# Attention and FP4 feed-forward in one kernel: a new order within the pairs of heads, fewer key tiles summed by GpSimd, and moved waits at a batch's end

## The chip, the cores and the metric

One core of one Trainium2 chip. The metric is the device time of one execution in microseconds, the median of several runs. The engines are TensorE (matmuls; PE, its weight loads PEld), VectorE (DVE), ScalarE (ACT), GpSimd (POOL) and SyncE (SP), which issues most DMAs.

## The reference

```python
# x: (8, 1024, 512) fp32, 16 heads of 32, F = 1408
xn  = layernorm(x)                                   # no scale, no shift, eps 1e-5
qkv = xn @ W_attn + b_attn
att = softmax(where(causal, q @ k.T * 32 ** -0.5, -inf))
x + (att @ v) @ W_proj + b_proj                      # attention
  + fp4(silu(fp4(xn) @ fp4(w_gate).T) * (fp4(xn) @ fp4(w_up).T)) @ fp4(w_down).T
# fp4: blocks of 16, scale = max|.| / 6, nearest of 0 .5 1 1.5 2 3 4 6
```

## The kernel before, in words

The kernel goes through eight batches of attention and then through a loop of 64 token tiles of the feed-forward part, which the change leaves as it is. fp32 products of accuracy are made of high and low halves in a rounded fp32 format.

A batch has three stages. First the projections (`PROJ`) make q, k and v; q and k go through DRAM and come back as stacks of a pair of heads. Then come eight pairs of heads. Then the end of the batch: the output projection (`output`), the additions (`add`), the quantisation of two of the feed-forward weight tiles beside it (`scale_unit`, `round_unit`, `transpose_unit`, `high_of_unit`, `low_of_unit`, `store_unit`), and the first four x tiles of the next batch (`transpose_x`, `low_of_x`).

A pair's work on TensorE, for eight key tiles of 128 keys:

- Row scores (`scores`, line 1189, step T): 16 tiles a pair, 128 queries by up to 1024 keys, whose row maxima VectorE takes (`row_max`, line 761). They are made for the pair ahead. Two may be under way. Their odd ones and the denominators share a bank.
- The step MAX (`maxima`, line 1194) transposes the maxima. VectorE splits them (`split_max`, lines 767 and 769), SyncE writes both halves into the pair's stack by two DMAs (line 521), and the pair's first transposed score waits for these (line 1209).
- Transposed scores (`transposed_scores`, line 1216, steps S0 to S3 of a row): keys by queries, with the maximum already subtracted. A row stands for one key tile and has 4 parts (rows 0 to 3), 2 (rows 4 and 5) or one for both heads (rows 6 and 7). They go round three banks: a part waits for the exp of the part three before. Parts on the diagonal get a mask matmul in bf16 (`mask_transposed`, lines 1225 and 1228, steps M). ScalarE takes exp (line 1066).
- Products with V (`times_v`, line 1242, steps P0 to P7, by key tile): four column tiles of the array at once, by head and by parity of the query tile. A key tile whose number isn't below its row's belongs to the pair before.
- Denominators (`denominators`, lines 1254 and 1261, step DEN, for the pair before): GpSimd sums the exps of key tiles (lines 686 and 688, `summed(p)` tiles of pair p); matmuls by ones sum over the keys, and the tiles that GpSimd leaves out are added by matmuls of ones on the exps themselves. VectorE copies the result (line 778), SyncE spreads it over the partitions (line 571), VectorE inverts (line 782), SyncE writes and broadcasts the inverse (lines 576 and 581), and VectorE divides (`divide`, line 798).

The order is written out by hand: `STEPS` has one string for each row on TensorE, gone through once per pair; `VECTOR_STEPS` is VectorE's order (R a row maximum, Y0 and Y1 the two halves of a division of the pair before last, DEN the copy, INV the inversion, MAX the split). Each engine works strictly in its order. A loop of a pair here is the time from its first transposed score to the next pair's.

```python
pe.wait_ge(m_in, ONE + b * PAIRS * 2 * DMA + (p + 1) * 2 * DMA)   # ahead of S0 of row 0
```

Of the kernel before, what the change touches and what calls it, by code (L numbers as in the profile page):

```python
# [45 lines left out]
def attention(nc, ctx, banks, memory, shared, x, w_attn, b_attn, w_proj, b_proj, w_gate, w_up, w_down, qk_scratch, ones_scratch,  # L46
# [5 lines left out]
    ST = S // P  # L52
    HG = P // HD
    G = HEADS // HG
    PAIRS = HEADS // 2
# [18 lines left out]
    ST_RING, SLOTS, XR, RES = 3, 4, 4, 6  # L74

    RINGED = 5
# [5 lines left out]
    TAIL0 = {kt: 2 * P * sum(ST - k for k in range(RINGED, kt)) for kt in range(RINGED, ST)}  # L82
    TAIL = 2 * P * sum(ST - k for k in range(RINGED, ST))

    def summed(p):

        return ST if p < PAIRS - 2 else RINGED if p < PAIRS - 1 else 3

    SUM_ORDER = [*range(1, ST)]
    FREED = {0: 1, 1: 1, 2: 2, 3: 3, 4: 4}
# [6 lines left out]

    STEPS = ["T T S0 S1 T P3 T S2 S3 T M2 M3",
# [7 lines left out]


    VECTOR_STEPS = "R R R R R R R Y0 Y1 DEN R R R R R R INV MAX R R R"
    FLAT = " ".join(STEPS).split()
    EARLY = TILES - FLAT[:FLAT.index("MAX")].count("T")

# [181 lines left out]
    SPLIT = G - 1  # L297
# [409 lines left out]
    def vector(dve):  # L707
# [46 lines left out]
        def body(b, final):  # L754
# [46 lines left out]
            def low_of_y(g):  # L801
                dve.wait_ge(y_hi, ONE + b * SPLIT * 2 + (g + 1) * 2)
                nc.vector.tensor_tensor(yt_low[:, g], yt[:, g], yt_high[:, g].bitcast(F32), ALU.subtract).then_inc(y_lo_first, 1)  # L803

            def add(k):

                if k >= 2:
                    dve.wait_ge(o_out[k % 2], ONE + b * (ST // 2) * DMA + (k // 2) * DMA)
                elif k == 0:
                    dve.wait_ge(y_div, ONE + b * PAIRS * 2 + PAIRS * 2)  # L810
                dve.wait_ge(o_res, ONE + b * ST + k + 1)
                filled(dve, b, "P", k)
                nc.vector.tensor_tensor(ob[:, k % 2], bank("P", k), res_tile(k, final), ALU.add).then_inc(o_sum, 1)
# [44 lines left out]
            def low_of_unit(i):  # L858
                n = turn(b, i)
                dve.wait_ge(q_out[i % 2], ONE + slot_turns(b, i) * 2 * DMA)  # L860
                dve.wait_ge(q_hi, ONE + n + 1)
                nc.vector.tensor_tensor(unit_space[i % 2][:, 4].bitcast(F32R), ps_y[:, :], unit_space[i % 2][:, 3],
                                        ALU.subtract).then_inc(q_lo, 1)
# [44 lines left out]
            for p in range(PAIRS):  # L908
                for step in VECTOR_STEPS.split():
                    if step == "R":  # L910
                        tile, due = tile_of(due), due + 1
                        if (1, AHEAD_OF_ALL) <= tile < (PAIRS, 0):
                            row_max(*tile)
                    elif step == "DEN":
                        if p:
                            copy_den(p - 1)
                    elif step == "INV":
                        if p == PAIRS - 1 and not final:

                            for g in range(SPLIT - 1):  # L920
                                low_of_y(g)
                        if p:
                            invert(p - 1)
                        if p == PAIRS - 1 and not final:
                            for t in range(XR):
                                norm(b + 1, t)
                        if p == PAIRS - 1 and final:

                            shared.quantise_first(dve)
                    elif step == "MAX":  # L930
                        if p + 1 < PAIRS:
                            split_max(p + 1)
                        if p == PAIRS - 2 and not final:
                            for t in range(XR):
                                stats(b + 1, t)
                    elif p > 1:
                        divide(p - 2, [int(step[1])])
# [1 line left out]
            invert_last()  # L939
            divide(PAIRS - 1)  # L940
            if not final:
                for t in range(XR):
                    low_of_x(b + 1, t)
            else:
                shared.low_of_first(dve)
            one, two = beside_projection(final)
            for k in range(ST):
                add(k)
                if k == 0:
                    scale_unit(one)  # L950
                if k == 1:
                    round_unit(one)
                if k == 2:
                    scale_unit(two)
                if k == 3:
                    round_unit(two)
                if k == 5:
                    low_of_unit(one)
                if k == 7:
                    low_of_unit(two)  # L960

        batches_in_line(body)

    def scalar(act):
# [16 lines left out]
        def body(b, final, rest):  # L981
# [11 lines left out]
            def high_of_unit(i):  # L993
                n = turn(b, i)
                act.wait_ge(q_out[i % 2], ONE + slot_turns(b, i) * 2 * DMA)
                act.wait_ge(q_full, ONE + n + 1)
                nc.scalar.activation(unit_space[i % 2][:, 3].bitcast(F32R), ps_y[:, :], ACT.Copy).then_inc(q_hi, 1)

            def store_unit(i):
                matrix, u = unit_of(b, rest, i)  # L1000
                act.wait_ge(q_lo, ONE + turn(b, i) + 1)
                for half in range(2):
                    act.dma_start(wq[half, :, matrix * FC + u], unit_space[i % 2][:, 3 + half]).then_inc(q_out[i % 2], DMA)

            for kind, i in PROJ:
# [19 lines left out]
                g, r, _ = QK[i]  # L1025
# [64 lines left out]
            one, two = beside_projection(final)  # L1090
            for k, t in enumerate(OUT):
                act.wait_ge(o_sum, ONE + b * ST + k + 1)
                act.dma_start(acc[b, t * P:(t + 1) * P, :], ob[:, k % 2]).then_inc(o_out[k % 2], DMA)
                if k + (2 if final else RES) < ST:
                    load(k + (2 if final else RES))
                if k == 0:
                    magnitudes(one)
                if k == 2:
                    magnitudes(two)
                if k == 4:  # L1100
                    high_of_unit(one)
                if k == 6:
                    high_of_unit(two)
                    store_unit(one)
            store_unit(two)

        batches_and_rest_in_line(body)

    def tensor(pe):
        pe.wait_ge(consts, 2)  # L1110

        def transpose_x(b, t):

            pe.wait_ge(t_lo, ONE + b * ST + max(t - ST_RING + 1, 0))
            pe.wait_ge(normed, ONE + b * ST + t + 1)
            for k in range(KC):
                last = nc.tensor.transpose(x_bank(t)[:, k * P:(k + 1) * P], xs[:, t % XR, k * P:(k + 1) * P],
                                           ident[:, :])
            last.then_inc(t_full, 1)
# [10 lines left out]
        def body(b, final):  # L1130
# [115 lines left out]
            def denominators(p):  # L1246
                pe.wait_ge(summed_up, ONE + b * SUMS + SUMS0[p] + summed(p) - 1)
                pe.wait_ge(first_sums, ONE + b * PAIRS + p + 1)
                if p + 2 < PAIRS:

                    pe.wait_ge(s_max, ONE + b * PAIRS * TILES + (p + 2) * TILES + AFTER_DEN // 2 * 2)
                for s in range(2):
                    for h in range(2):
                        last = nc.tensor.matmul(by_tile(den_bank(p)[y_rows(h, s)]), ones[:, :], by_tile(sums(p, h, final))[:, s::2],  # L1254
                                                start=True, stop=summed(p) == ST)
                for kt in range(summed(p), ST):
                    for s in range(2):
                        if parity_tiles(kt, s) >= ST:
                            continue
                        for h in range(2):  # L1260
                            last = nc.tensor.matmul(by_tile(den_bank(p)[y_rows(h, s), y_cols(kt, s)]), ones[:, :],
                                                    exps_of_parity(kt, h, s), start=False, stop=kt == ST - 2 + s)
                last.then_inc(den_full, 1)
# [79 lines left out]
            for k in range(OUT_BANKS):  # L1343
                pe.wait_ge(y_div, ONE + b * PAIRS * 2 + (PAIRS - 2 + min(k, 1)) * 2)
                emptied("P", k)
                output(k, range(G - 1))
            if not final:
                transpose_x(b + 1, XR - 1)
            pe.wait_ge(y_div, ONE + b * PAIRS * 2 + PAIRS * 2)
            one, two = beside_projection(final)  # L1350
            for k in range(ST):
                if k < OUT_BANKS:
                    output(k, [G - 1])
                else:
                    emptied("P", k)
                    output(k, range(G))
                if k == 4:
                    transpose_unit(one)
                if k == 6:
                    transpose_unit(two)  # L1360

        batches_in_line(body)

# [452 lines left out]
```

## Time and profile before

| what | value |
| --- | --- |
| median of 3 runs | 3576.71 us (3575.12 to 3578.76) |
| profiled execution | 3577.77 us, span 3575.8 us |
| granted TensorE clock | 0.999 of full speed |
| TensorE busy | 3510.3 us (98%) |
| VectorE busy | 2688.8 us (75%) |
| ScalarE busy | 1217.6 us (34%) |
| GpSimd busy | 1103.0 us (31%) |

The shares are over the whole span. The eight batches take about 2016 us of it, the feed-forward loop the rest; GpSimd works in the first part alone. Matmuls are pipelined and their ends are modelled, so the time that a step takes on TensorE is read from the starts of two neighbours. A wait is put down to the instruction whose signal came last.

### The profile page before, as it was taken

To read this page: it belongs to the slowest core of one execution; us is meant where nothing else is said; L and a number is where in the kernel's file an instruction comes from. 1 tells how busy PE (TensorE), PEld (TensorE's weight loads), DVE (VectorE), ACT (ScalarE), POOL (GpSimd) and SP (SyncE) were. 2 spreads that over 40 slices of the span, in tenths; PEclk is the share of its full clock that TensorE was granted. 3 is DMA by queue.
4 is the path that set the end of the run, shared out by engine and by line. 5 is a ranking of instruction groups with operands and counts; after the bars stand their busy time and mean duration, and the time that the engine had idled before them with its cause. 6 is when DMAs were issued, how large, how long until landed. Compare 5 with 4: busy or idle time off the path is not lost.

```text
span 3575.8 us, 55225 instructions
## 1 busy us (share of the span) xinstructions
PE 3510.3 (98%) x19892; PEld 2607.0 (73%) x19892; DVE 2688.8 (75%) x4872; ACT 1217.6 (34%) x2292; POOL 1103.0 (31%) x552
## 2 busy tenths in 40 slices
PE   8999999999999999999999999999999999999999
PEld 6557567566576575675665688888888888888887
DVE  6786876877877768778777677777777777777776
ACT  2542543534615525435335222222222222222222
POOL 1770952934817709529338100000000000000000
PEclk9999999999999999999999999999999999999999
DMA  6535446346365355363465410110110110110010
GB/s 220 133 100 188 105 146 172 83 154 170 82 197 133 109 180 116 134 183 83 139 189 161 177 32 29 35 35 27 35 35 26 35 35 28 34 35 31 31 35 30
DMA packets 182895, 348.94 MB, mean 98 GB/s; under 512 B 42960, under 2 KB 50640, under 8 KB 181840
## 3 DMA queue, kind: packets, MB, share of 16 engines
q1 hardware_dynamic: 158256, 291.75, 28.4%
q10 hardware_dynamic: 24480, 55.06, 4.3%
q8 instruction: 101, 1.65, 0.2%
q14 instruction: 58, 0.48, 0.0%
HBM read 225.19 MB, written 120.00 MB: 97 GB/s over the span
## 4 chain that ended last, share of the span: by engine, by line
PE 78%; DVE 6%; issue 6%; POOL 3%; DMA 3%; ACT 2%; SPq 1%; ACTq 0%; POOLq 0%; DVEq 0%
PE f_ps L1691 27%; PE f_ps_o L1703 13%; PE ps_dense L1164 12%; PE ps_st L1216 6%; PE ps_s L1189 5%; PE ps_dense L1242 3%; PE ps_y L1242 3%; POOL stage L688 2%; PE ps_dense L1254 2%; PE f_ps L1683 2%; PE ps_dense L1189 1%; POOL stage L686 1%; DVE yt_low L803 1%; PE ps_dense L1330 1%; PE ps_st L1225 1%
## 5 line engine op out<-in xcount | busy, mean ns | idle before, releaser
L1691 PE MATMUL f_ps<-wgu,xqt 128*128 128x512 f32 (+1 forms) x4608 | 990.2, 372 | 1.7 <-DVE xqt L1546 1.4
L1691 PEld LDWEIGHTS f_ps<-wgu,xqt 128*128 128x128 f32 x4608 | 840.4, 188 | 122.7 <-DVE xqt L1546 1.6
L1066 ACT ACTIVATE pt<-ps_st 128x512 f32<-128x512 f32 (+3 forms) x1152 | 543.6, 525 | 448.8 <-PE ps_st L1216 306.8
L761 DVE CUSTOM_DVE_ANT_0 ps_s<-ps_s,row_mask 128x640 f32<-128x640 f32 (+3 forms) x512 | 529.9, 1035 | 126.8 <-PE ps_s L1189 122.6
L1703 PE MATMUL f_ps_o<-wd,hqt 128*128 128x512 f32 x2112 | 512.1, 395 | 0.6 <-DVE hqt L1572 0.6
L1703 PEld LDWEIGHTS f_ps_o<-wd,hqt 128*128 128x128 f32 x2112 | 392.0, 188 | 79.4 <-DVE hqt L1572 0.8
L1164 PE MATMUL ps_dense<-arena,wa 128*128 128x512 f32 x1536 | 378.2, 395 | 0.3 <-DVE stage L818 0.3
L686 POOL TENSOR_TENSOR stage<-pt 128x1792 f32<-128x1792 f32 x41 | 164.9, 4021 | 564.2 <-ACT pt L1066 546.0
L1164 PEld LDWEIGHTS ps_dense<-arena,wa 128*128 128x128 f32 x1536 | 284.8, 188 | 60.9 <-issue 3.8
L688 POOL TENSOR_TENSOR stage<-stage,pt 128x1536 f32<-128x1536 f32 (+2 forms) x107 | 321.4, 3004 | 15.7 <-ACT pt L1066 8.2
L1216 PE MATMUL ps_st<-arena 98*128 98x512 f32 (+3 forms) x768 | 247.4, 390 | 4.7 <-ACT pt L1066 2.2
L761 DVE CUSTOM_DVE_ANT_0 ps_dense<-ps_dense,row_mask 128x128 f32<-128x128 f32 (+3 forms) x424 | 219.0, 516 | 40.0 <-PE ps_dense L1189 38.2
L1216 PE MATMUL ps_st<-stack 98*128 98x512 f32 (+3 forms) x768 | 242.9, 382 | 3.2 <-DMA stack<-mr 2.6
L1636 ACT ACTIVATE silu<-f_ps 128x512 f32<-128x512 f32 (+1 forms) x192 | 107.1, 558 | 369.3 <-PE f_ps L1691 369.2
L1216 PEld LDWEIGHTS ps_st<-arena 98*128 98x128 f32 x768 | 136.6, 191 | 88.6 <-ACT pt L1066 46.0
L1631 ACT ACTIVATE ha<-ht 128x1408 f32<-128x1408 f32 x63 | 87.1, 1382 | 325.2 <-DVE ht L1467 325.2
L1028 ACT ACTIVATE stage<-ps_dense,bqk 128x512 fp32r<-128x512 f32 x128 | 88.0, 688 | 314.0 <-PE ps_dense L1164 297.6
L1565 DVE TENSOR_TENSOR h<-silu,f_ps 128x512 f32<-128x512 f32 (+1 forms) x192 | 122.7, 639 | 92.1 <-ACT silu L1636 88.6
L1164 PE MATMUL ps_dense<-wa,arena 128*128 128x512 f32 x768 | 187.5, 394 | 0.0
L1216 PEld LDWEIGHTS ps_st<-stack 98*128 98x128 f32 x768 | 138.2, 192 | 66.2 <-ACT pt L1066 30.3
L1470 DVE SCALAR_TENSOR_TENSOR hd<-ha,ht 128x1408 f32<-128x1408 f32 (+1 forms) x65 | 104.2, 1603 | 91.9 <-ACT ha L1631 91.2
L818 DVE SCALAR_TENSOR_TENSOR stage<-ps_dense,bqk,stage 128x512 fp32r<-128x512 f32 x128 | 95.9, 749 | 101.6 <-ACT stage L1028 101.6
(166 smaller groups left out, 5425.1 us busy)
## 6 DMA issues: line engine op xcount, KB each, us to landing
qk_scratch<-stage SPq DMA_DIRECT2D x128, 512.0 KB, 3.0
stack<-qk_scratch SPq DMA_DIRECT2D x192, 256.0 KB
arena<-qk_scratch SPq DMA_DIRECT2D x192, 256.0 KB
xs<-in_L_attn_x SPq DMA_DIRECT2D x64, 256.0 KB, 3.8
acc_scratch<-rob ACTq DMA_DIRECT2D x64, 256.0 KB, 2.0
xt<-in_L_attn_x SPq DMA_DIRECT2D x64, 256.0 KB, 2.6
at<-acc_scratch SPq DMA_DIRECT2D x64, 256.0 KB, 2.7
out<-ot SPq DMA_DIRECT2D x64, 256.0 KB, 2.0
```

The source lines that it names most:

```text
L686: nc.gpsimd.tensor_tensor(both[:, :, cols], exps(0)[:, :, cols], exps(1), ALU.add).then_inc(summed_up, 1)
L688: nc.gpsimd.tensor_tensor(both[:, :, cols], both[:, :, cols], exps(kt), ALU.add).then_inc(summed_up, 1)
L761: nc.vector.tensor_tensor_reduce(row, row, row_mask[:, S - keys:S], -1.0, LARGEST, ALU.add, ALU.min, mx[:, h * ST + q:h * ST + q + 1]).the ...
L1066: nc.scalar.activation(exps(kt)[:, heads[0], q - kt * P:q - kt * P + n], ps_st[:, w % ST_RING, 0:n], ACT.Exp, scale=SCALE).then_inc(st_exp, 1)
L1164: last = nc.tensor.matmul(bank(*use), left(lh, k), right(rh, k), start=n == 0, stop=n == len(terms) - 1)
L1189: last = nc.tensor.matmul(out[:, k0:k1], qs, stack(p)[0:KS, 2 + h, k0:k1], start=True, stop=True)
L1216: last = nc.tensor.matmul(ps_st[:, w % ST_RING, j * n:(j + 1) * n], stack(p)[0:KM, 2 + h, kt * P:(kt + 1) * P], stack(p)[0:KM, h, q:q + n] ...
L1242: last = nc.tensor.matmul(by_tile(y_bank(p)[y_rows(h, s), y_cols(kt, s)]), v_head(kt, p, h), exps_of_parity(kt, h, s), start=kt == 0, stop ...
L1565: nc.vector.tensor_tensor(h[:, f:f + n], silu[:, c, 0:n], ps[:, SLOT[c], 1, 0:n], ALU.mult).then_inc(h_mul, 1)
L1636: nc.scalar.activation(silu[:, c, 0:n], ps[:, SLOT[c], 0, 0:n], ACT.Silu).then_inc(s_done, 1)
L1691: last = nc.tensor.matmul(ps[:, SLOT[c], gu, 0:n].rearrange("p (j n) -> p j n", n=P), xqt[:, a, k], wgu[:, b, gu * FC + f // P:gu * FC + ( ...
L1703: last = nc.tensor.matmul(ps_o[:, :], hqt[:, a, k], wd[:, b, k], start=i == 0, stop=i == len(terms) - 1)
```

## The change

It writes `STEPS` and `VECTOR_STEPS` anew. MAX goes from the end of row 3 to the start of row 5, DEN from row 2 to the start of row 3, the products of P3 and P4 of the pair before go together at the end of row 0, P5, P6, P7 in row 1, and the row-score tiles T are spread otherwise: three come behind MAX where five did. GpSimd sums 8, 7, 8, 7, 7, 6, 5, 3 key tiles in the pairs 0 to 7 instead of 8, 8, 8, 8, 8, 8, 5, 3. At the end of a batch VectorE makes only one of its two low halves of y ahead of the last inversion from DRAM, the fourth x tile's transposition and low half come after the first output tile, and the second weight tile's transposition and its halves move behind the eight outputs; the first one's halves are taken one step earlier.

```diff
+    SUMMED = (8, 7, 8, 7, 7, 6, 5, 3)
     def summed(p):
-        return ST if p < PAIRS - 2 else RINGED if p < PAIRS - 1 else 3
+        return SUMMED[p]

-    STEPS = ["T T S0 S1 T P3 T S2 S3 T M2 M3",
-             "S0 P5 T T S1 S2 S3 M2 M3 T",
-             "S0 DEN P6 P7 P0 S1 T S2 S3 T M2 M3 T P1 T T",
-             "S0 S1 P2 S2 M2 S3 M3 MAX",
-             "S0 T M0 S1 M1",
-             "S0 T M0 S1 T M1",
-             "S0 P4 M0",
-             "S0 M0"]
-    VECTOR_STEPS = "R R R R R R R Y0 Y1 DEN R R R R R R INV MAX R R R"
+    STEPS = ["S0 S1 S2 M2 T S3 T M3 P3 P4 T",
+             "T S0 S1 S2 T P5 P6 P7 M2 T S3 M3",
+             "S0 T S1 S2 T S3 M2 M3",
+             "DEN P0 T T S0 S1 S2 P1 T T M2 S3 M3",
+             "S0 T M0 S1 M1 P2",
+             "MAX S0 T M0 S1 M1",
+             "S0 M0 T",
+             "S0 M0 T"]
+    VECTOR_STEPS = "R R R R Y0 R R R Y1 R DEN R R R R R INV MAX R R R"
...
 # VectorE, step INV of the last pair, not in the final batch
-                            for g in range(SPLIT - 1):
-                                low_of_y(g)
+                            low_of_y(0)
                         if p:
                             invert(p - 1)
                         if p == PAIRS - 1 and not final:
+                            for g in range(1, SPLIT - 1):
+                                low_of_y(g)
                             for t in range(XR):
                                 norm(b + 1, t)
...
 # VectorE, end of the batch
-                for t in range(XR):
+                for t in range(XR - 1):
                     low_of_x(b + 1, t)
...
             for k in range(ST):
                 add(k)
+                if k == 0 and not final:
+                    low_of_x(b + 1, XR - 1)
...
-                if k == 5:
+                if k == 4:
                     low_of_unit(one)
-                if k == 7:
-                    low_of_unit(two)
+            low_of_unit(two)
...
 # ScalarE
-                if k == 4:
+                if k == 3:
                     high_of_unit(one)
                 if k == 6:
-                    high_of_unit(two)
                     store_unit(one)
+            high_of_unit(two)
             store_unit(two)
...
 # TensorE, denominators
-                                                start=True, stop=summed(p) == ST)
+                                                start=True, stop=summed(p) >= ST - 1 + s)
...
 # TensorE, output projection
-            if not final:
-                transpose_x(b + 1, XR - 1)
...
+                if k == 0 and not final:
+                    transpose_x(b + 1, XR - 1)
                 if k == 4:
                     transpose_unit(one)
-                if k == 6:
-                    transpose_unit(two)
+            transpose_unit(two)
```

## Rows read from the trace of the kernel before

**Rows 1.** the page: busy us of each engine (share of the span), instructions
```profile
PE 3510.3 (98%) x19892; PEld 2607.0 (73%) x19892; DVE 2688.8 (75%) x4872; ACT 1217.6 (34%) x2292; POOL 1103.0 (31%) x552
```

**Rows 2.** windows, batch 2: us; busy PE, PEld, DVE, ACT, POOL (count); clock, DMA, GB/s
```profile
611.57:630.30 18.73, 17.93 (x133) 10.07 (x132) 13.74 (x37) 10.44 (x24) 17.64 (x9) 1.00 0.60 135
648.17:666.04 17.87, 17.87 (x133) 10.01 (x132) 15.17 (x39) 10.46 (x24) 16.62 (x8) 1.00 0.46 107
...
701.75:719.31 17.56, 16.82 (x125) 8.85 (x124) 14.56 (x42) 11.72 (x27) 16.52 (x8) 1.00 0.25 71
...
739.10:767.90 28.80, 26.58 (x113) 18.98 (x114) 22.86 (x33) 4.63 (x8) 10.06 (x8) 1.00 0.59 203
```

**Rows 3.** waits of the whole span: engine and line, releaser; us in total, times, longest
```profile
PEld ps_s L1189 <- DVE mx L761: 109.3, 205, 0.8
...
PE ps_dense L1254 <- POOL stage L688: 8.7, 14, 1.4
```

**Rows 4.** timeline of TensorE, pair loop 3 of batch 2: start us, us, instructions
```profile
649.74 0.73 PE L1189 MATMUL ps_s<-stack 96*128 96x512 f32 x2
650.31 0.64 PE L1216 MATMUL ps_st<-arena 98*128 98x512 f32 x2
650.78 0.23 PE L1189 MATMUL ps_dense<-stack 96*128 96x128 f32 x1
...
654.25 1.07 PE L1254 MATMUL ps_dense<-stage,ones 128*32 128x512 f32 x8
655.13 0.62 PE L1242 MATMUL ps_dense<-rob,v 128*32 128x128 f32 x12
...
661.73 0.28 PE L1194 MATMUL ps_dense<-ident,mx 128*128 128x128 f32 x1
...
662.08 0.45 PE L1189 MATMUL ps_s<-stack 96*128 96x512 f32 x2
662.37 0.23 PE L1225 MATMUL ps_st<-identb,causal 128*128 128x128 bf16 x1
...
662.77 0.42 PE L1216 MATMUL ps_st<-arena 98*128 98x384 f32 x1
...
664.47 0.64 PE L1242 MATMUL ps_y<-pt,v 128*32 128x256 f32 x8
665.04 0.28 PE L1228 MATMUL ps_st<-identb,causal 128*128 128x256 bf16 x1
...
665.38 0.42 PE L1189 MATMUL ps_dense<-stack 96*128 96x384 f32 x1
...
666.04 0.63 PE L1216 MATMUL ps_st<-stack 98*128 98x512 f32 x2
```

**Rows 5.** timeline of VectorE and of SyncE, same loop; DMA issues: KB, us to landing
```profile
662.04 0.28 DVE L767 CAST mr<-ps_dense 16x128 fp32r<-16x128 f32 x1 [0.35 <-PE ps_dense L1194]
...
656.26 3.08 SPq L571 DMA_DIRECT2D den<-rob  x4
...
662.66 1.17 SPq L521 DMA_DIRECT2D stack<-mr  x2
...
stack<-mr SPq DMA_DIRECT2D x64, 8.0 KB, 2.1
arena<-mr SPq DMA_DIRECT2D x64, 8.0 KB, 1.8
```

**Rows 6.** timeline of TensorE, pair loop 6 of batch 2
```profile
715.86 0.28 PE L1194 MATMUL ps_dense<-ident,mx 128*128 128x128 f32 x1
...
719.30 0.50 PE L1216 MATMUL ps_st<-arena 98*128 98x512 f32 x1
```

**Rows 7.** timeline of ScalarE, pair loop 3 of batch 2
```profile
657.09 0.60 ACT L1066 ACTIVATE pt<-ps_st 128x512 f32<-128x512 f32 x1 [2.05 <-PE ps_st L1216]
```

**Rows 8.** timeline of VectorE and of TensorE at the end of batch 1
```profile
480.02 7.31 DVE L803 TENSOR_TENSOR yt_low<-yt,stack 128x1024 fp32r<-128x1024 f32 x2
...
517.07 0.66 PE L1201 MATMUL ps_y<-ident,pt 128*128 128x128 f32 x4 [1.32 <-DVE pt L862]
```

## The prediction

> **What bounds the kernel now.** I read the engine shares first: TensorE is busy 98% of the span, VectorE 75%, GpSimd 31% [rows 1]. The reader should see that only time that TensorE gains or loses can move the end. The change touches the attention part alone, so next I read windows cut at the starts of the pairs' transposed scores, in batch 2: pair loop 1 takes 18.73 us, a steady loop (3) 17.87 with TensorE busy in all of it, loop 6 17.56, the batch's end, from the last denominators to the next batch's first product, 28.80, of which TensorE is busy 26.58 [rows 2]. The waits come third: TensorE's largest are weight loads of row scores behind a row maximum (109.3 us in 205 waits, mostly hidden under the matmul before) and denominators behind GpSimd's sums (8.7 us in the open) [rows 3]. Last the timeline of one steady pair, because a busy share can't say how near a hidden wait is to showing [rows 4, 5].
>
> **The chain that the new order uncovers.** A pair's first transposed score needs the row maxima: the transposition MAX on TensorE, cast and subtraction on VectorE, two DMAs issued one behind the other by SyncE, their landing. In the steady pair MAX starts at 661.73 [rows 4], the cast at 662.04, the first DMA is issued at 662.66, and both issues take 1.17 us, so the second starts 0.59 later [rows 5]. A DMA from mr lands 1.8 us (arena slots) or 2.1 us (stack slots) after its issue in the median [rows 5]. Sum: 0.93 + 0.59 + 1.8 to 2.1 = 3.3 to 3.6 us. The next pair's S0 starts at 666.04, 4.31 us after MAX, so some 0.8 us of cover is left over. Loop 6 shows the chain bare: MAX at 715.86, S0 at 719.30, 3.44 us, with less work behind MAX [rows 6]. I take 3.5 us: this, and a little for a weight load that waits itself and then shows.
>
> The Trainium skill (DMA: Bandwidth & Descriptors, the section on the two cost components of a DMA) gives a fixed cost of about 2.0 us whatever the size. By that figure, as an estimate, the chain is 0.2 us longer than with the arena row's 1.8 and the sum below some 10 us higher; loop 6's bare chain speaks against it, and I don't use it.
>
> In the old order MAX closes row 3. In the new one it opens row 5, behind row 4's scores, masks and P2. What stood behind MAX and no longer does, by the starts in the steady pair [rows 4]: S4.0, S4.1 and their masks 0.72 (from 661.76, just behind MAX, to 662.77, less T0, 662.08 to 662.37), P4 0.57 (664.47 to 665.04) and 0.10 for entering it, and the row-score tiles T3 and T4 0.66 (665.38 to 666.04), which the new order puts behind S0. 4.31 - 2.05 = 2.26 us of work is left against a chain of 3.5: TensorE stands 1.24 us before each pair. Nothing can pass the waiting S0: all of TensorE's later work is queued behind it, and with it the exps, the row maxima and the sums. 3.4 us is the least that the wait's end can come after MAX by these rows; with traffic a landing can be later.
>
> **What the new order saves.** (a) One visit to the V products fewer (6 to 5: P3 P4, P5 P6 P7, DEN P0, P1, P2); the column work of the visits together is the same. A visit's edges: DEN, two passes of 512 columns, takes 0.88 (654.25 to 655.13), so P4's two passes of 256 are 0.44, and it takes 0.57: 0.13 to leave it. The first tile behind a visit takes 0.57 for 1024 columns (649.74 to 650.31) where two other scores of 512 take 0.47 (650.31 to 650.78): 0.10, since its weights load in the open. I take the same 0.10 for V's weights at the visit's start. Together 0.33 us a pair [rows 4]. (b) 205 weight loads wait for a row maximum, over three a pair [rows 3]; where such a load shows it costs that 0.10. The new places give VectorE more time ahead of most tiles and part the two divisions: some 0.3 to 0.4 a pair. (c) Against that, new waits. S0.3 stands three scores behind S0.0 and needs its exp: 0.4 for the score to end, 0.6 for an exp of 512 columns [rows 7] and 0.1 of signals and load, against 1.0 us of work between: 0.1. T11 needs the copy of the denominators, which had P6, P7, P0 and S2.1 as cover and now has P0 alone: up to 0.1. Net of (a), (b), (c), with a little for fewer masks ahead of scores: 0.6 us saved, between 0 (all of (b) comes back as other waits, and some of (a)) and 0.95.
>
> A steady loop: 17.87 - 0.6 + 1.24 = 18.5, so +0.63 us.
>
> **GpSimd's sums.** Pairs 1, 3 and 4 leave out key tile 7, pair 5 tiles 6 and 7; TensorE adds them as matmuls of ones. Two passes of 128 columns are 0.22 by DEN's 0.88 for 512 [rows 4]; tile 7 is one such, tiles 6 and 7 two: 3 x 0.22 + 0.44 = 1.1 us a batch, all on the path, since DEN stands ahead of MAX. GpSimd is busy 16.6 of 17.87 us in a steady pair [rows 2], which an 18.5 us pair relieves anyway, so I count nothing won there (0 to -0.2 a pair). What goes is DEN's wait for GpSimd in loop 1, as DEN stands some 2 us later: loop 1 is 0.86 over the steady one [rows 2], and 8.7 us of such waits in 8 batches [rows 3] agree with it: -0.85 a batch.
>
> **Sum of the pairs, per batch.** Loops 1 to 5: 5 x 0.63 = 3.15. Ones: 1.1. DEN in loop 1: -0.85. Loop 0: the 0.72 of row 4 comes ahead of MAX and the 4.3 behind it shrinks to 3.5: 0. Loop 6 was bound by the chain before, so all that moves ahead of MAX or behind S0 counts: 0.72 + 0.67 + 0.66 - 0.6 = +1.45. Loop 7 gets P4 of pair 6 and is bound by exps otherwise: +0.3 (0 to 0.6). Late landings, which 0.8 us of cover used to hide: 0.06 a pair, 0.4. Together 5.5 us a batch, 44 us in 8.
>
> **The batch's end.** (d) VectorE makes one low half of y, then the inversion, then the other. Both took 7.31 us ahead of the inversion (from 480.02) [rows 8], which now comes some 3 us earlier, and with it the division of pair 6, the last reciprocal, the last division and the first addition, the latter by 1 to 2 us, until the last denominators bind. (e) The fourth x tile's transposition no longer stands between the first output groups and the last, and the second unit's transposition goes behind output 7: its wait of 1.32 us for the first unit's low half (517.07) [rows 8] goes, as that low half also comes one addition earlier. TensorE idles 2.2 us in this stage (28.80 - 26.58) [rows 2]; I take 1.8 back in 7 batches and 1.0 in the last: -13.6 us. The bounds are 0 and -18. That the second unit's high and low halves now end later, ahead of the next batch's first copies on ScalarE and VectorE, costs nothing while the next batch's first products (12 matmuls of 512 columns, 2.8 us by the 0.47 for two) cover them; without that cover it costs 1 us a batch.
>
> Total: 44 - 13.6 = +30.4 us on the profiled execution's 3577.8 (span 3575.8), 3608.2. The median of the runs shown is 1.1 below that execution: 3607 us.
>
> **Rivals.**
> 1. The first score doesn't wait: the maxima land sooner, or TensorE's work behind MAX is longer than I count. A steady pair is then 17.27 us and a batch 5 x -0.6 + 1.1 - 0.85 + 0.3 = -2.5; 8 x -2.5 - 13.6 = -34: 3543 us. For it: one visit fewer, and TensorE is the bound. Against it: loop 6 has this very wait now. It decides from a chain below 2.3 us; the total breaks even at one of 2.95. Chance 0.06.
> 2. VectorE is held at the inversion when MAX comes. From DEN to MAX there is 6.9 us of work in the new order (DEN and P0 1.9, T11 and T12 0.75, S3.0 to P1 1.8, T13 and T14 0.7, S3.3 to the last mask of row 4 1.0, P2 0.78). The denominators' first DMA is issued 2.0 us after DEN's start (656.26), the four issues take 3.08 us [rows 5], a landing some 1.8: 6.3 to 6.9. Where these are late the cast waits, and S0 with it: 0.3 to 0.5 us in half of the pairs, 10 to 15 us in all: 3620 us. Chance 0.14.
> 3. The savings cover the wait: 0.95 a pair (-17 us), all of 18 at the batch's end, loop 7 unchanged (-2): 44 - 17 - 2 - 18 = +7: 3583 us. Chance 0.05.
> The forecast itself: 0.75.
>
> **Numbers.** Range 3585 to 3630: the lower end by savings of 0.95 a pair and some more at the batch's end, the upper by savings near 0.2 a pair (+19) or rival 2. No change is within 0.2%, 7 us, about what a measurement of this kernel can tell. Faster 0.06, same 0.04, slower 0.90.
>
> **What would show it.** From MAX to the next pair's first score 3.4 to 3.6 us in every pair, TensorE idle for some 1.2 us there and the wait put down to the DMA from mr; steady loops of 18.3 to 18.7; a loop 6 near 19; no wait of DEN for GpSimd; more idle time on GpSimd and VectorE per pair; a batch's end near 27 us without the 1.3 us ahead of the unit's transposition. I am wrong if that first score starts at once, or if steady loops come under 17.9.

## The result and the profile after

The changed kernel takes 3666.3 us (median of 4 runs, 3662.9 to 3672.4) against 3577.0 for the kernel before beside it: ratio 1.0252, interval 1.0234 to 1.0269. It is slower, as forecast, but by 89 us and not by 30, outside the range of 3585 to 3630. The profiled execution took 3672.4 us, 94.6 more than that of before.

The page has the busy us of each engine, then the granted clock in 40 slices. TensorE has 192 matmuls more than in [rows 1], of 128 columns each, and is busy 39 us longer. The row of the granted clock shows a 9 in every slice, as that of the kernel before does, so the page hides what happened:

```profile
PE 3549.2 (97%) x20084; PEld 2664.6 (73%) x20084; DVE 2682.3 (73%) x4872; ACT 1217.0 (33%) x2292; POOL 1072.1 (29%) x512
...
PEclk9999999999999999999999999999999999999999
```

The windows answer to [rows 2]. Batch 5 is the one in which only loop 7 was disturbed. In order: loops 1, 2, 3, 6, 7 and the end of batch 5, then loops 2 and 3 of batch 2, and a stretch of 3.2 us in batch 1 (columns as in [rows 2]; the granted clock is the third number from the right):

```profile
1420.51:1439.09 18.58, 17.59 (x132) 10.39 (x132) 13.94 (x38) 10.46 (x23) 17.55 (x9) 1.00 0.59 132
1439.09:1457.91 18.82, 17.81 (x136) 10.71 (x136) 15.01 (x40) 10.46 (x23) 16.16 (x7) 1.00 0.44 101
1457.91:1476.84 18.93, 17.60 (x132) 10.39 (x132) 15.16 (x40) 10.46 (x23) 16.74 (x8) 1.00 0.43 100
1514.60:1534.15 19.55, 17.54 (x139) 10.18 (x139) 15.07 (x44) 12.42 (x27) 17.48 (x7) 1.00 0.23 70
1534.15:1555.54 21.39, 21.06 (x207) 11.63 (x208) 10.72 (x15) 11.28 (x25) 13.05 (x6) 0.92 0.30 99
1555.54:1582.78 27.24, 27.09 (x115) 19.28 (x116) 23.51 (x34) 4.03 (x7) 10.10 (x8) 1.00 0.58 203
...
660.53:680.93 20.40, 19.40 (x135) 11.26 (x135) 15.01 (x40) 10.46 (x23) 16.13 (x7) 0.92 0.40 93
680.93:701.43 20.50, 19.16 (x132) 10.91 (x132) 15.18 (x40) 10.46 (x23) 16.73 (x8) 0.92 0.39 93
...
385.60:388.80 3.20, 3.20 (x19) 1.75 (x20) 1.48 (x4) 0.60 (x1) 3.04 (x3) 0.50 1.04 225
```

The same loop 2 takes 18.82 us at a clock of 1.00 and 20.40 at 0.92. The last row shows where such a mean comes from: for 3.4 us the clock is granted at half, the 1.2 GHz level, and 3.4 x 0.5 / 20.4 is the 8% that loop 2 lacks. The pair loops of this trace hold 30 such stretches, of 3.4 us or twice that, 119 us in all; those of the kernel before hold none.

The waits of the whole span (us, times, longest) answer to [rows 3]. The new ones are the 32 + 24 = 56 first scores, and the weight loads behind the copy of the denominators. The 205 weight loads of row scores into ps_s that waited for a row maximum have become 9; those into ps_dense, 41 before, are 90:

```profile
PE ps_st L1217 <- DMA arena<-mr: 44.4, 32, 3.1
PE ps_st L1217 <- DMA stack<-mr: 28.9, 24, 3.0
...
PEld ps_dense L1190 <- DVE mx L761: 64.4, 90, 0.8
...
PEld ps_s L1190 <- DVE mx L761: 6.2, 9, 1.7
...
PEld ps_dense L1190 <- DVE rob L778: 48.6, 48, 1.3
...
PE ps_dense L1190 <- DVE rob L778: 2.9, 8, 0.4
```

TensorE's timeline of pair loop 3 in batch 5 answers to [rows 4]: denominators, P0, the tile behind it (T11), MAX, the last tile ahead of the next pair, and the next pair's first score:

```profile
1466.19 1.06 PE L1255 MATMUL ps_dense<-stage,ones 128*32 128x512 f32 x8
1467.08 1.04 PE L1243 MATMUL ps_y<-pt,v 128*32 128x512 f32 x8
1468.48 0.45 PE L1190 MATMUL ps_dense<-stack 96*128 96x384 f32 x1 [0.36 <-DVE rob L778]
...
1473.39 0.33 PE L1195 MATMUL ps_dense<-ident,mx 128*128 128x128 f32 x1
...
1475.28 0.60 PE L1190 MATMUL ps_s<-stack 96*128 96x512 f32 x2
1476.84 0.96 PE L1217 MATMUL ps_st<-stack 98*128 98x512 f32 x3 [0.96 <-DMA stack<-mr]
```

From MAX to the first score it is 3.45 us, as worked out, with 0.96 us of idle time at its end. VectorE and SyncE in the same loop, which answer to [rows 5]: a row maximum, the denominators' copy, the cast behind MAX, the DMAs:

```profile
1466.76 0.97 DVE L761 CUSTOM_DVE_ANT_0 ps_s<-ps_s,row_mask 128x768 f32<-128x768 f32 x1
...
1467.74 0.69 DVE L778 COPY rob<-ps_dense 128x512 f32<-128x512 f32 x1
...
1473.76 0.28 DVE L767 CAST mr<-ps_dense 16x128 fp32r<-16x128 f32 x1 [0.44 <-PE ps_dense L1195]
...
1474.38 1.17 SPq L521 DMA_DIRECT2D stack<-mr  x2
```

Last, the same visit P3 at both clock levels: in batch 5, and in batch 2, 2.66 us behind a first score (680.93) that had waited 0.96 us:

```profile
1460.10 1.28 PE L1243 MATMUL ps_dense<-pt,v 128*32 128x256 f32 x16
```
```profile
680.93 0.96 PE L1217 MATMUL ps_st<-arena 98*128 98x512 f32 x3 [0.96 <-DMA arena<-mr]
...
683.59 2.36 PE L1243 MATMUL ps_dense<-pt,v 128*32 128x256 f32 x16
```

**Where the 94.6 us are.** An undisturbed batch is 148.8 us from its first score to its last denominators (15.34, 18.58, 18.82, 18.93, 18.82, 18.94, 19.55, and 19.85 for loop 7, which the fill run below shows at full clock) against 142.8 before: 6.05 x 8 = 48. The batch's end, to the next batch's first score, went from a mean of 104.7 to 102.8 us in seven batches: -13.6 in sum. Clock: a disturbed loop 2 is 1.58 us longer (20.40 - 18.82) for its 3.4 us at the low level; 119 / 3.41 x 1.58 = 55. The rest, 5, is about what late first scores leave: in this trace they came, in sum, 13.6 us later than 3.45 us after MAX, and the kernel before has some 6 us of longer loops of its own. My terms were 44, -13.6, none, and 3 within the 44. The 55 is an estimate, as it prices every low stretch like that of loop 2.

### The profile page after: what moved, and what is told of

It reads as the page before. It is cut to its first block, busy times and chain, and to the rows that moved or that the text cites. A ratio compares the mean times of both kernels' runs of the same rounds, so it can differ in the third digit from the quotient of the medians.

```text
span 3670.6 us, 55494 instructions
## 1 busy us (share of the span) xinstructions
PE 3549.2 (97%) x20084; PEld 2664.6 (73%) x20084; DVE 2682.3 (73%) x4872; ACT 1217.0 (33%) x2292; POOL 1072.1 (29%) x512
## 4 chain that ended last, share of the span: by engine, by line
PE 86%; DVE 6%; DMA 4%; issue 2%; ACT 1%; SPq 1%; ACTq 0%; POOL 0%; POOLq 0%; DVEq 0%
PE f_ps L1691 26%; PE ps_dense L1165 14%; PE f_ps_o L1703 13%; PE ps_st L1217 7%; PE ps_dense L1243 4%; PE ps_s L1190 4%; PE ps_y L1243 4%; PE ps_dense L1331 3%; PE ps_dense L1190 2%; DMA arena<-mr 2%; PE f_ps L1683 1%; DMA stack<-mr 1%; PE ps_st L1226 1%; PE ps_dense L1255 1%; DVE ps_s L761 1%
## 5 line engine op out<-in xcount | busy, mean ns | idle before, releaser
L1217 PE MATMUL ps_st<-stack 98*128 98x512 f32 (+3 forms) x768 | 234.4, 383 | 31.3 <-DMA stack<-mr 28.9
L1217 PEld LDWEIGHTS ps_st<-arena 98*128 98x128 f32 x768 | 144.8, 200 | 109.0 <-DMA arena<-mr 53.7
L1217 PEld LDWEIGHTS ps_st<-stack 98*128 98x128 f32 x768 | 145.6, 197 | 71.8 <-DMA stack<-mr 36.7
L1226 PE MATMUL ps_st<-identb,causal 128*128 128x128 bf16 x768 | 166.2, 234 | 0.0
```

What stands on the lines that cost most here:

```text
L1217: last = nc.tensor.matmul(ps_st[:, w % ST_RING, j * n:(j + 1) * n], stack(p)[0:KM, 2 + h, kt * P:(kt + 1) * P], stack(p)[0:KM, h, q:q + n] ...
L1226: nc.tensor.matmul(ps_st[:, w % ST_RING, 0:P], causal[:, :], identb[:, :], start=False, stop=True).then_inc(st_full, 1)
```

## The experiments

**Fill the wait.** Does the low clock make the missing 60 us? Five matmuls of 512 columns run ahead of each pair's first score, into its own bank, which the score then overwrites. They need nothing that the score waits for but its bank, so the order and the landing stay as they are (MAX to the first score is 3.49 us).

```diff
                 w = p * NPARTS + PART0[kt] + i
+                if (kt, i) == (0, 0) and p:
+                    pe.wait_ge(st_exp, ONE + b * PAIRS * NPARTS + max(w - ST_RING + 1, 0))
+                    for _ in range(5):
+                        nc.tensor.matmul(ps_st[:, w % ST_RING, 0:512], stack(p)[0:KS, 2, 0:P], stack(p)[0:KS, 0, 0:512],
+                                         start=True, stop=True)
```

> The changed kernel, with five matmuls of 512 columns (1.15 us of TensorE) put ahead of each pair's first transposed score, into the bank which that score then overwrites: TensorE works through most of the 1.2 us in which it waited for the row maxima, and nothing gets there sooner. Theory A (the clock): the wait itself costs what was forecast, some 34 us with everything else in, and the rest of the 89 us, some 55, is the granted clock falling behind that wait. Then the granted clock comes back to 0.998 or more, steady loops are all 18.8 to 18.9 us, and the time is about 3612 us, 0.985 of the changed kernel, although TensorE has more to do. Rival B (the new order itself is longer on TensorE, or the clock falls for another reason): the time stays near 3666 us or rises by up to 60 us, and the clock stays near 0.985.

Measured: 3621.5 us (3619.5 to 3628.1), ratio 1.0123 (1.0106 to 1.0139). More work on TensorE made the kernel 45 us faster. The windows of loops 3 and 6 of batch 5 are within 0.1 us of those in the changed kernel, and the clock is full:

```profile
1426.67:1445.60 18.93, 18.56 (x137) 11.26 (x137) 15.17 (x40) 10.46 (x23) 16.78 (x8) 1.00 0.43 100
1483.36:1502.84 19.48, 18.71 (x144) 10.98 (x144) 15.01 (x44) 12.42 (x27) 17.45 (x7) 1.00 0.21 70
```

10.2 us at the low level are left in the pair loops, of 119. So the wait's length and the clock are two costs, and this takes away the second alone. The time is 9 us above the expected 3612; the stretches that are left make about 5 of them (10.2 / 3.41 x 1.58).

**The batch's end alone**, on the kernel before: the edits to low_of_y, low_of_x, transpose_x, high_of_unit, low_of_unit and transpose_unit, with all key tiles summed as before.

```diff
-            if not final:
-                transpose_x(b + 1, XR - 1)
...
+                if k == 0 and not final:
+                    transpose_x(b + 1, XR - 1)
                 if k == 4:
                     transpose_unit(one)
-                if k == 6:
-                    transpose_unit(two)
+            transpose_unit(two)
```

> The kernel before with the edits at the batch's end alone (old order, old sums). Theory A: 1.8 us less per batch end, 7 batches and about 1 us in the last: -13 us, 3564 us, clock 0.999. Rival: the end's later halves of the second weight tile delay the next batch's first copies, and the gain is under 4 us.

Measured: 3565.9 us (3561.3 to 3568.2), ratio 0.9968 (0.9955 to 0.998): -11.8 us against -13.6 worked out. The batch's end in batch 2, of 28.80 us in [rows 2], is

```profile
733.61:760.84 27.23, 27.01 (x115) 19.26 (x115) 22.02 (x31) 4.04 (x7) 10.04 (x8) 1.00 0.57 201
```

**A late maximum in the old order.** Three small DMAs to scratch in memory, issued by SyncE ahead of the two that the first score waits for, lengthen the chain and leave TensorE's order alone.

```diff
                 sp.wait_ge(m_lo, ONE + b * PAIRS + p + 1)
+                for j in range(3):
+                    sp.dma_start(mx_scratch[j], mr[:, j % 2].bitcast(F32)).then_inc(mx_out, DMA)
```

> The kernel before in its old order, with three more small DMAs (to a scratch in DRAM) issued ahead of the two that carry the row maxima: each takes the queue some 0.59 us, so the chain from MAX to the next pair's first score is some 5.2 us long against 4.3 us of cover. One suspected cost alone, without the new order. Theory A: the wait of some 0.9 us in loops 0 to 5 and 1.8 more in loop 6 makes 7.2 us a batch, 58 us at full clock (3635 us), and the granted clock falls behind such waits too, so 3650 to 3700 us at a clock of 0.98 to 0.99. Rival B (the clock falls for something in the new order, not for the wait): 3635 us at 0.998.

Measured: 3625.5 us (3618.3 to 3638.1), ratio 1.0129 (1.0112 to 1.0146). The three issues cost less than I took: MAX to S0 became 4.69 us, so a steady loop waits only 0.2 us. A batch of this trace at full clock throughout (the fourth) is 2.4 us longer than the same batch of the kernel before, so by its length the longer chain is worth 2.4 x 8 = 19 us. Of the 60 us by which the profiled execution is longer, the low level makes another 33, by the same price: 71.7 us in 9 stretches of up to 10.2 us. The remaining 8 lie in loops with later first scores. A loop at full clock and one with such a stretch:

```profile
664.28:682.60 18.32, 18.02 (x131) 9.94 (x132) 15.25 (x40) 10.45 (x23) 16.67 (x8) 1.00 0.46 106
623.45:646.09 22.64, 22.42 (x131) 12.09 (x132) 12.74 (x35) 10.56 (x23) 16.59 (x8) 0.77 0.49 109
```

The 31 first scores with a wait under 0.5 us never lowered it. Each stretch begins in or behind a wait of 1.0 to 1.8 us: seven times that of a late first score or of the one at loop 6's end, twice that of a row score for VectorE. The one above began 1.1 us behind this score:

```profile
623.45 0.73 PE L1220 MATMUL ps_st<-stack 98*128 98x512 f32 x2 [1.31 <-DMA stack<-mr]
```

**The same with two fill matmuls** ahead of each first score.

```diff
+                if (kt, i) == (0, 0) and p:
+                    ...
+                    for _ in range(2):
+                        nc.tensor.matmul(ps_st[:, w % ST_RING, 0:512], ...)
```

> e3's kernel (old order, maxima 0.4 us late for S0) with two matmuls of 512 columns (0.46 us) ahead of each pair's first transposed score. The chain and the loops stay as in e3 where the clock is full (18.22 us). Theory A: TensorE is no longer idle there, and the granted clock goes from 0.989 to 0.998 or more: the 72 us at the lower clock in e3's attention part cost about half, 30 to 36 us, less where they lay over waits, so 3590 to 3605 us. If the clock fell for another reason: 3625 us at 0.989.

Measured: 3619.4 us (3610.7 to 3622.5), ratio 1.0119 (1.0104 to 1.0135). By the medians the fill wins 6 us only, as the late maximum's runs differ much (and lie over this run's 3610.7 to 3622.5 in part): 3638.1, 3628.8, 3622.2 and 3618.3 us at mean clocks of 0.989, 0.992, 0.994 and 0.996. The profiled executions are the fastest of the one and the slowest of the other, so their difference is no measure of the edit, but it fits the price of the low level: 3610.7 us with 6.8 us at the low level against 3638.1 with 71.7, -27 us, where 64.9 / 3.41 x 1.58 = 30 were due. A steady loop and loop 7 of batch 5, the latter with the same 19.47 us as without the fill:

```profile
1389.83:1408.05 18.22, 18.22 (x135) 10.37 (x134) 15.03 (x39) 10.45 (x23) 16.61 (x8) 1.00 0.46 105
1481.10:1500.58 19.48, 19.36 (x199) 10.14 (x200) 11.29 (x10) 11.26 (x25) 12.95 (x6) 1.00 0.30 102
```

So the two matmuls fill the short waits to the end, cost nothing in a steady loop, and leave the length of the late chain as it is. As the short waits had not lowered the clock, what helps must be the longer ones: the wait at loop 6's end went from 1.10 to 0.64 us. With 6 us between the medians, this pair of runs supports the account of the clock by its traces and hardly by its times.

**P4 moved alone, five visits.** What is a visit to the V products worth?

```diff
-    STEPS = ["T T S0 S1 T P3 T S2 S3 T M2 M3",
+    STEPS = ["T T S0 S1 T P3 P4 T S2 S3 T M2 M3",
...
-             "S0 P4 M0",
+             "S0 M0",
```

> The kernel before with one edit: P4 moved from row 6 behind P3 in row 0 of the next loop, so that a pair has five visits to the V products, while MAX keeps 3.6 us of work behind it. If a visit's edges cost what I took (0.33 us a pair on the path), this is 56 x 0.33 = 18 us less, 3560 us. Rival C (the steady pair is held by the alternation of row scores and row maxima, so that time saved on TensorE elsewhere turns into a longer wait for VectorE at the next row-score tiles): less than 4 us of change, and more waiting of L1189 for L761.

Measured: 3586.3 us (3580.7 to 3590.4), ratio 1.0026 (1.0016 to 1.0036). That is 9 us more than the kernel before, where 18 less were expected. An undisturbed batch is 0.4 us longer, 3 us in eight; the profiled execution is the fastest of nine, the others stand at mean clocks down to 0.996, and what lengthens them was not traced. A steady loop is 17.91 us, none the shorter, and busy throughout:

```profile
648.65:666.56 17.91, 17.91 (x132) 10.36 (x132) 15.25 (x39) 10.35 (x23) 16.55 (x8) 1.00 0.46 107
```

Rival C of that expectation holds in its mechanism, though not in its size (under 4 us of change). P4's 0.67 us are gone from behind MAX, but MAX to S0 went from 4.31 to 4.06 only, because the tile ahead of the next pair waits for VectorE. VectorE's third row maximum behind MAX ends at 666.00, and the tile that needs its bank starts at 666.06 and not 0.25 us after the one before it, as in the kernel before (665.63, behind the 665.38 of [rows 4]):

```profile
664.98 0.97 DVE L761 CUSTOM_DVE_ANT_0 ps_s<-ps_s,row_mask 128x768 f32<-128x768 f32 x1
665.86 0.14 DVE L761 DVE_READ_ACCUMULATOR2_ANT mx<- 128x1 f32 x1
```
```profile
665.64 0.42 PE L1189 MATMUL ps_dense<-stack 96*128 96x384 f32 x1
666.06 0.67 PE L1189 MATMUL ps_s<-stack 96*128 96x512 f32 x2
```

The hidden waits of weight loads grew from 205 to 248 in number, with the same total ([rows 3]: 109.3 us):

```profile
PEld ps_s L1189 <- DVE mx L761: 108.7, 248, 0.8
```

**The order alone**: the new STEPS and VECTOR_STEPS on the kernel before, nothing else.

```diff
-             "S0 S1 P2 S2 M2 S3 M3 MAX",
+             "DEN P0 T T S0 S1 S2 P1 T T M2 S3 M3",
...
+             "MAX S0 T M0 S1 M1",
```

> The kernel before with the new STEPS and VECTOR_STEPS alone (old sums, old batch end). If the batch's end gives 12 us back wherever it stands, as e2 showed in the old order, and the sums of seven tiles cost 1.1 us a batch (9 us): 3666 + 12 - 9 = 3669 us, clock 0.984. If the sums cost nothing, since the ones fall where TensorE would wait for VectorE or for the maxima anyway: 3678 us.

Measured: 3679.7 us (3674.0 to 3687.7), ratio 1.0287 (1.0271 to 1.0303), 116 us at the low level in the pair loops. The order carries the whole loss, and the batch's end takes back its 12 us in the full change.

**The change with eight tiles summed** on GpSimd in all of pairs 0 to 5.

```diff
-    SUMMED = (8, 7, 8, 7, 7, 6, 5, 3)
+    SUMMED = (8, 8, 8, 8, 8, 8, 5, 3)
```

> The changed kernel with GpSimd summing all eight tiles in pairs 0 to 5, as before. My step: 1.1 us of ones a batch are on the path, so this is 9 us faster, 3657 us. Rival: the time is the same within 3 us (steady loops 18.82 and 18.93 as in the changed kernel), or it is slower, because DEN now waits for GpSimd's eighth sum.

Measured: 3676.7 us (3669.9 to 3681.9), ratio 1.0281 (1.0266 to 1.0297). I had expected it faster by the ones' matmuls; it isn't. At full clock loops 2 and 3 are 18.81 and 18.95 us here, both without ones; in the changed kernel, where loop 2 has them, they are 18.82 and 18.93. Loop 6 is 19.12 instead of 19.53. The low level has 130 us of this trace's pair loops instead of 119, which by 1.58 per 3.41 is 5 us; that and the rest of the 10 may be chance, as the profiled executions of the two are equal (3672.8 and 3672.4). The windows above say why the loops are equal: loop 2 with one tile of ones has 136 matmuls and 17.81 us busy, loop 3 without has 132 and 17.60. The ones' 0.21 us lie in time for which T11 waits for the copy anyway. Without them that wait is in the open 33 times and not 8:

```profile
PE ps_dense L1190 <- DVE rob L778: 10.3, 33, 0.4
```

**The high half first.** In the changed kernel SyncE waits for both halves of the row maxima before it issues either DMA. This one issues the high half's as soon as the cast is done.

```diff
-                sp.wait_ge(m_lo, ONE + b * PAIRS + p + 1)
                 for j in range(2):
+                    sp.wait_ge([m_hi, m_lo][j], ONE + b * PAIRS + p + 1)
```

> The changed kernel with the DMA of the maxima's high halves issued when these are made, and not with the low halves': the chain from MAX to the next pair's first score is 0.3 us shorter, 3.15 us, and so is the wait. Theory A: 0.3 us x 55 pairs = 17 us at full clock, and the granted clock falls in fewer places: 3625 to 3650 us, clock 0.985 to 0.995. If the clock doesn't depend on the wait: 3649 us at 0.984. If the chain isn't what ends the wait: 3666 us.

Measured: 3611.8 us (3607.6 to 3614.8), ratio 1.01 (1.0085 to 1.0116). MAX to S0 is 3.13 us. The same loop 3 of batch 5:

```profile
1406.18:1424.78 18.60, 17.57 (x131) 10.38 (x132) 15.16 (x39) 10.46 (x23) 16.72 (x8) 1.00 0.43 102
```

The shorter wait is worth 0.3 x 56 = 17 us by itself. The kernel won 54, since only 37.5 us of the 119.5 at the low level are left: (119.5 - 37.5) / 3.41 x 1.58 = 38. None of these stretches begins behind one of the 45 first scores that waited some 0.65 us. Eight of the nine stand behind waits of 1.25 us or more, six of them at loop 7's first score, which waits 1.41 us here in most batches; the ninth is in a loop 0, behind two waits of 0.77 and 0.41.

**P1 beside P0**, to give T11 the cover that it lacks.

```diff
-             "DEN P0 T T S0 S1 S2 P1 T T M2 S3 M3",
+             "DEN P0 P1 T T S0 S1 S2 T T M2 S3 M3",
```

> The changed kernel with P1 moved next to P0 in row 3, so that T11's wait for the copy of the denominators (0.4 us a pair in the changed kernel, behind P0 alone) lies under P1, and a pair has four visits. If that wait is what ate the savings: up to 0.4 + 0.3 us a pair, steady loops of 18.2 to 18.4, and MAX to S0 still 3.45. Against it VectorE's alternation with the row scores (e4): T13 and T14 now follow T12 with less between them and wait longer for row maxima, and the loops stay at 18.8 or longer. The wait ahead of S0 is the same either way, so the clock stays near 0.985 and the time is 3630 to 3690 us.

Measured: 3698.1 us (3695.7 to 3710.1), ratio 1.0347 (1.0331 to 1.0363). T11 no longer waits, and two tiles later the wait is back, longer, behind a row maximum; it was 9 times and 4.7 us in the changed kernel:

```profile
1502.34 0.44 PE L1190 MATMUL ps_dense<-stack 96*128 96x384 f32 x1
...
1504.55 0.74 PE L1190 MATMUL ps_s<-stack 96*128 96x512 f32 x2 [0.65 <-DVE mx L761]
```
```profile
PE ps_s L1190 <- DVE mx L761: 41.5, 65, 1.1
```

**A version that beats both.** The batch's end alone and the high half first; and the same with seven tiles summed in pair 0, for DEN's wait in loop 1.

> e2's kernel (old order and sums, new batch end) with the high halves' DMA issued early as in e7. The chain is hidden in loops 0 to 5 except where a landing is late; loop 6 was bound by it (3.4 us): 0.2 to 0.3 us a batch there, and as much where landings are late, some 0.5 us a batch: 4 us less than e2, 3562 us, the fastest version so far.

> e8's kernel with GpSimd summing seven tiles in pair 0 alone. Loop 1 is 18.75 us in e8 against 17.85 for the others, because DEN waits 0.8 us there for GpSimd; a tile of GpSimd's is 0.73 us. Loop 1 becomes 18.1 to 18.2 us if tile 7's ones cost 0.2 us on the path, 18.0 if nothing: 0.6 to 0.7 us a batch, 5 us, 3559 us and the fastest version. Rival: the wait of loop 1 isn't for the last sum, and nothing changes (3564 us).

Measured: 3563.7 us (3561.1 to 3564.2), ratio 0.9961 (0.9947 to 0.9974), and 3565.2 (3559.4 to 3567.6), ratio 0.9963 (0.995 to 0.9977). Both are 13 us faster than the kernel before beside them, and neither can be told from the other, nor the first from the batch's end alone (3565.9) with certainty. In the trace with seven tiles loop 1 of batch 2 takes

```profile
607.83:625.98 18.15, 18.10 (x136) 10.23 (x136) 13.70 (x37) 10.44 (x24) 16.89 (x8) 1.00 0.64 145
```

instead of 18.73 in [rows 2], but the medians don't show it.

## Why the prediction was wrong, by its own steps

**The chain** of 3.5 us: right, 3.45 us in nearly every pair. The work left behind MAX was 2.5 us (3.45 - 0.96) and not 2.26, so the wait is 0.96 and not 1.24. That it ends at S0 and is put down to the DMA from mr is as forecast, 56 times.

**The step that failed** is the one that turned the wait into time: "TensorE stands 1.24 us before each pair", with a price of the 1.24 us alone. It put the clock at nothing, without a reason. The sum took every other instruction's duration from a trace at full clock [rows 2] and so assumed that the clock stays. With a wait of about 1 us in each pair the granted clock fell to the 1.2 GHz level 30 times for 3.4 us or more, and that is 55 of the 64 us by which the profiled execution passed the forecast (3672.4 against 3608.2). The fill shows it from one side, the high half first from the other, and the late maximum shows it in the old order. [rows 2] could not have shown it: its loops, the 0.74 us of idle time in loop 6 included, all stand at 1.00. Yet the prediction had no term, no rival and no width for it.

The Trainium skill (TensorE: Matmul & The Clock Gate, the section on the HAM clock gate) says that the throttled state is the default and that activity releases it, and also that for modelling the penalty of the ramp at a kernel's start is under 1% of a typical kernel's span. The first agrees with the fill. The second is no price for what happened here: the 55 us are 1.5% of the span, and all of them come from falls in mid-stream, where TensorE is 95% busy.

**The savings (a) and (b)**, 0.6 us a pair: mis-sized. TensorE's busy time in loop 3 fell from 17.87 to 17.60 us, 0.27. P4 moved alone saved nothing. The old loop was not only bound by TensorE: VectorE's row maxima and TensorE's row scores take turns, and in that run the edge that was taken out came back as a wait for a row maximum, in the weight load where the waits view shows it as hidden. That the same held for the rest of (a) and (b) in the new order is argued from it, and no run here takes them apart. I had that as the lower bound ("all of (b) comes back as other waits, and some of (a)") and took the value near the upper.

**(c) T11**, up to 0.1 us: it is 0.36 in loop 3, where TensorE stands idle for it, 8 times in all; in loops 2 and 4 ones take most of its place. The copy of the denominators is queued on VectorE behind a row maximum until 1467.74, half a microsecond after DEN ends, and runs for 0.69. I had looked at the cover on TensorE and not at VectorE's queue. So this loop is 17.60 + 0.96 + 0.36 = 18.92 us, and the forecast of 18.5 had 17.27 + 1.24 + 0.

**The ones**, 1.1 us a batch: 0.4. Those of tile 7 in pairs 1, 3 and 4 fall into T11's wait, those of pair 5 cost 0.41 in loop 6. The two errors together leave the pairs' sum near its forecast: 6.05 us a batch against 5.5.

**DEN's wait in loop 1** went as said (18.58, below the other loops). **Loop 6** was 19.55 against "near 19" and the 0.44 of its ones: right. **Loop 7**: no change at full clock, not +0.3. **The batch's end**: 27.24 us for "near 27"; the wait ahead of the unit's transposition is gone; -13.6 us in seven batches, -11.8 in all when made alone, for -13.6 in all.

**Rival 2** did not decide: VectorE is 0.44 us idle ahead of the cast in the rows above. Rivals 1 and 3 fell with the wait.

What stays open is which waits lower the clock. Counted over the first scores of loops 1 to 7 in all 13 traces, with a fall put down to a wait if the low level began between the wait's start and 3 us behind its end:

| wait of the first score | first scores | falls |
| --- | --- | --- |
| none | 327 | 0 |
| under 0.5 us | 68 | 2 |
| 0.5 to 0.85 us | 68 | 0 |
| 0.85 to 1.05 us | 168 | 54 |
| 1.05 to 1.6 us | 34 | 16 |
| over 1.6 us | 63 | 61 |

So the length counts for much, and a step of 0.3 us from 0.96 to 0.65 took the falls behind the steady loops' waits away altogether. But it does not decide alone. The two falls under 0.5 us are both in the run with P4 moved alone, in loop 7, behind two idle stretches of 0.13 to 0.29 us each. In the kernel before, between 100 and 2100 us, TensorE waits 0.9 to 1.7 us eleven times outside the pair loops (1.32 us ahead of a unit's transposition in [rows 8], for one), and the clock stays full. Of the 40 waits of about 0.96 us in the changed kernel 14 lowered it, and these come in series: 662.0, 682.5, 703.0 and 723.4 us are four falls in a row in batch 2, while batch 5, with the same waits, has none before loop 7. And P1 beside P0, whose steady loops have the most idle time (1.6 us, in two waits), had 92 us and not more than the changed kernel's 119.

## What to carry to other kernels

A wait on a nearly always busy TensorE is not worth its length alone: where an edit opens one of about a microsecond in every iteration, work out the time at full clock and again with the low level in a good part of the iterations, and let the range reach there. Read the granted clock of windows, not of the page, before anything else is explained. And an edge saved on one engine counts only if the engine that it takes turns with was early; test it alone before it pays for something else.

## What the runs showed of the hardware that was not expected

- The granted clock fell to the 1.2 GHz level within a stretch where TensorE was 93% busy (loop 3: 17.60 of 18.93 us), each time for 3.4 us or a multiple of it, beginning up to 2.3 us behind a first score that had waited 0.96 us. It costs 1.58 us for each 3.4 us here.
- 1.2 us of matmuls without use ahead of each first score took 109 us of the low level away, and 45 us of time.
- A chain 0.3 us shorter (one DMA issued before its twin's data is ready) was worth 54 us where the clock was falling, and 2 us, which is within the noise, where it was not. A wait of 0.65 us lowered the clock in none of 45 loops, one of about 0.96 in 14 of 40, one of 1.7 or more in all 15 of the changed kernel.
- Both DMAs from mr landed 1.8 us after their issue in the median of the changed kernel, the stack's no later than the arena's.
